# Graph attention on one core: the transposes of the next tile's codes move from before the first unit to after the second

## The reference

```python
# layer 0: h0 = relu(layernorm(x)); two rounds of attention over the neighbours
Wh = h @ W_l
e = leaky_relu(u + v.T + c, 0.2)          # u, v: one number per row
att = softmax(where(adj > 0, e, -9e15), axis=1)
h = 0.2 * h0 + 0.8 * elu(att @ Wh)        # twice, with W[0] and W[1]
x = x + concat([h0, h1, h2]) @ mlp_w + mlp_b
# layer 1: the mean of the neighbours
h = relu(layernorm(x));  a = (adj == 1)
x = x + concat([a @ h / a.sum(1), h]) @ weight + bias
```

## Time and profile before

| what | us |
|---|---|
| median of 3 runs | 1790.13 |
| lowest and highest | 1787.9, 1791.51 |
| the profiled execution | 1792.32 |
| its span, first to last instruction | 1790.5 |

### The profile page before, as it was taken

One profiled execution on the slowest core, in us unless ns is written; L12 is line 12 of the kernel. 1 busy time (PEld: TensorE's weight loads), 2 busy tenths in 40 slices (PEclk: granted clock), 3 DMA queues, 4 the chain that ended last, 5 costly groups with the idle time before them and its releaser, 6 DMA issues. The chain is left out here.

```text
span 1790.5 us, 50269 instructions
## 1 busy us (share of the span) xinstructions
PE 1545.7 (86%) x21779; PEld 1495.5 (84%) x21779; DVE 1565.8 (87%) x2551; ACT 1249.3 (70%) x1341; POOL 144.9 (8%) x164
## 2 busy tenths in 40 slices
PE   2247698888888888888959999999999999799998
PEld 1237688788787878887849999999999999799998
DVE  7689999999999999999989859688696888986675
ACT  3266589898888888888768999999999996000000
POOL 1370000010101010101051000000000000000000
PEclk9668999999999999999979999999999999999999
DMA  7938899999999999999311111111211211133231
GB/s 243 239 144 307 337 362 389 373 380 391 376 405 361 407 367 404 360 407 356 151 43 45 56 44 49 39 59 43 61 55 37 60 31 43 54 102 96 84 96 49
DMA packets 114238, 353.93 MB, mean 198 GB/s; under 512 B 9056, under 2 KB 17248, under 8 KB 114016
## 3 DMA queue, kind: packets, MB, share of 16 engines
q1 hardware_dynamic: 92064, 304.50, 45.5%
q0 software_dynamic: 8512, 27.33, 5.7%
q10 hardware_dynamic: 13440, 18.88, 2.9%
HBM read 323.35 MB, written 27.33 MB: 196 GB/s over the span
## 5 line engine op out<-in xcount | busy, mean ns | idle before, releaser
L475 ACT ACTIVATE region<-ub,bigv 128x1024 uint8<-128x1024 f32 x1024 | 1099.3, 1150 | 81.1 <-DMA x_d<-region 30.9
L1445 PE MATMUL bank<-wsplit,region 128*128 128x195 bf16 x8192 | 791.0, 250 | 62.6 <-DVE region L791 53.8
L1445 PEld LDWEIGHTS bank<-wsplit,region 128*128 128x128 fp8e3 x8192 | 696.6, 99 | 76.4 <-DVE region L791 40.5
L1451 PE MATMUL bank<-wsplit,region 128*128 128x130 f16 x8192 | 558.3, 221 | 58.2 <-DVE region L799 56.9
L1451 PEld LDWEIGHTS bank<-wsplit,region 128*128 128x128 fp8e3 x8192 | 500.5, 98 | 87.7 <-DVE region L799 87.4
L799 DVE SCALAR_TENSOR_TENSOR region<-region 128x512 uint32<-128x512 uint32 x512 | 346.0, 694 | 21.7 <-PE bank L1451 21.0
L791 DVE SCALAR_TENSOR_TENSOR region<-region 128x512 uint32<-128x512 uint32 x512 | 343.1, 699 | 1.4 <-ACT region L475 1.3
L811 DVE TENSOR_SCALAR region<-region 128x4096 uint8<-128x4096 int32 x128 | 293.4, 2292 | 0.1
L1660 PE MATMUL bank<-wsplit,region 128*128 128x129 f16 x4096 | 243.3, 222 | 11.1 <-DVE region L1277 11.1
L1660 PEld LDWEIGHTS bank<-wsplit,region 128*128 128x128 fp8e3 x4096 | 241.0, 99 | 12.6 <-DVE region L1277 12.6
L1277 DVE TENSOR_SCALAR region<-region 128x512 uint32<-128x512 uint32 x256 | 100.4, 424 | 42.7 <-PE bank L1660 37.6
(11 more groups left out here) (183 smaller groups left out, 742.8 us busy)
## 6 DMA issues: line engine op xcount, KB each, us to landing
region<-in_adj SPq DMA_DIRECT2D x128, 2048.0 KB, 11.0
region<-codes_d SPq DMA_DIRECT2D x128, 256.0 KB, 2.7
codes_d<-region ACTq DMA_DIRECT2D x64, 256.0 KB, 6.3
ub<-u_d POOLq DMA_DIRECT2D x16, 512.0 KB, 5.8
hg<-h_d POOLq DMA_DIRECT2D x16, 256.0 KB, 4.8
region<-in_x SPq DMA_DIRECT2D x4, 512.0 KB, 6.3
h_d<-wsplit POOLq DMA_DIRECT2D x4, 512.0 KB, 4.3
x_d<-region POOLq DMA_DIRECT2D x8, 256.0 KB, 16.0
```

What stands on the lines that cost most here:

```text
L475: last = nc.scalar.activation(sv[:, b, :], ub[G % 2][:, :], ACT.Relu, bias=bigv[l][:, t:t + 1], scale=BIG)
L1445: return nc.tensor.matmul(acc_on[it], columns(onb[U % NS], it, b), wsplit[:, c * TC + 2 * q + b, 0:WC], start=(c == 0 and q == 0 and b == ...
L1451: return nc.tensor.matmul(acc_off[it], columns(offb[U % NO], it, b), woff[:, c * TC + 2 * q + b, WO:WO + WF], start=(c == 0 and q == 0 and ...
```

## The change

It moves one call, in the loop over the first layer's tiles. Nothing is added or removed.

```diff
                 for n in range(NT):
                     g, r = n // NCH, n % NCH
+                    unit(0, n, 0)
+                    unit(0, n, 1)
                     if n + 1 < NT:
                         transpose_codes(n + 1)
-                    unit(0, n, 0)
-                    unit(0, n, 1)
                     if n == 1 or (g > 0 and r >= 5) or (g > 1 and r == 0):
                         if n + 1 < NT:
                             pe.wait_ge(p_in, n + 2)
```

## The result

The changed kernel takes 1799.5 us (median of 4, 1799.1 to 1799.9), the kernel before 1789.6 beside it; the ratio is 1.0055, with a 95% interval of 1.0038 to 1.0073. That is 0.4 to 0.7% slower, 6.8 to 13.1 us. The span of the profiled execution grew from 1790.5 to 1798.0 us, 7.5, where the sum said 7.1.

A forecast was written before the change was run, and what follows sets the result against it. VectorE was taken to bound the first layer; 4.9 us at the group ends plus 2.2 at the layer's end gave 7.1, so 1790.1 + 7.1 = 1797.2 us, with 8 in 10 for 1791.5 to 1804.

The forecast's parts named there:

- the sum: Whole kernel: 4.9 us at seven group ends plus 2.2 at the layer's end, 7.1 us slower.
- What bounds: First layer: VectorE sets the time, its waits are paid in full, and at most some 1.3 us can be won.
- The ordinary tile: Most first-layer tiles: later transposes cost nothing, with 3.7 us to spare for the codes and 2.3 for pack_pairs.
- The new wait: 27 tiles: PE resumes 1.73 us after its transposes begin, once ScalarE has copied; 21 cost nothing, except the last two.
- The end of a group: Seven group boundaries: ScalarE reaches the accumulators late, so pack_pairs is 0.73 us late; 0.7 a time, 4.9 in all.
- the boundary is absorbed: Group ends, rival: scaled_sums before E + 0.8 means no pack_pairs wait, only +2.2 at the layer's end, 1792.3; chance 0.24.
- the first wait: Group's first tile: VectorE waits 0.73 us before pack_pairs, hiding a second wait, 0.4 us, for the take of the codes.
- The upper bound: Group ends: ScalarE's copies take 1.6 us longer beside PE's matmuls, 2.3 us a boundary or 16 in all.
- the forecast's lower end: Forecast total with a cost of 0.25 us a boundary: 1793.7 us, in a case given 0.66.
- The end of the layer: Tiles 62 and 63: PE's lag of 0.46 us and a new wait of 1.73 are paid, 2.2 us.
- The clock: Rival: new waits in PE bring its clock down, 1.6 us each; 34 us slower, 1824; chance 0.07.
- The rival's price: Lowered clock in tiles r = 5, 6, 7, 0: 5.7 us less slack of 1.9, or 3.8 a group.

The follow-up runs named there:

- e5: Changed kernel with the old order in the last tile of each group, the first of the next, and tile 62; ratio 1.0007 to the kernel before.
- e3: Changed kernel with the old order in the first tile of each group but the first group; ratio 1.0029 to the kernel before.
- e2: Kernel before, with the new order only in the last tile of each group and the first of the next; ratio 1.0026 to the kernel before.
- e1: Kernel before, with the new order in tile 62 alone; ratio 1.0008 to the kernel before.
- e7: Changed kernel, but ScalarE copies out the small product of r = 0 after emptying the accumulators, not before; ratio 1.0031 to the kernel before.
- e6: Changed kernel with the old order in tile 62 alone; ratio 1.0042 to the kernel before.
- e4: Changed kernel with the old order in the last tile of each group (r = 7); ratio 1.0011 to the kernel before.
- e8: Changed kernel with the next tile's transposes moved between the first and second unit, in all tiles; ratio 1.0007 to the kernel before.

## Why the prediction was right

*What bounds.* Right. VectorE is the clock of this layer, and every idle of it shows in the total: eight idles before line 822 with 0.08 added to each, 5.7 us, and 0.2 at a DMA make up the 5.9 by which the tiles grew.

*The ordinary tile.* Right, in e5: no cost, with all distances in place. ScalarE's idle moved from before line 496 to before line 483.

*The new wait.* Its size was right: 1.12 us at r = 5 to 7, with line 1403 starting 1.72 after the transposes (1.73 said). So was the lag: in tile 39 the transposes came 6.07 into the tile (606.31, with its start at 600.24, 11.02 before 611.26), said 6.04. One place was left out: at r = 0 PE waits longer, 1.94, because ScalarE is late there.

*The end of a group.* Right in mechanism, and in size at six boundaries: they are 0.74 late, said 0.73. That it is so near is luck in part. ScalarE reached the accumulators at E + 1.38, where I had 1.50, and the boundary is absorbed before E + 0.65, where I had E + 0.8; the two errors, 0.1 each, cancel. The take began at E + 10.01 (said 10.37) and ended at 11.15, under the first wait, as said. Without the first wait, in e3, it cost 0.17 to 0.22.

The upper bound, 2.3 a boundary, had 1.6 us in it that last_units lost at one boundary and not at another (4.52 - 2.89), added to ScalarE's copies. With the new order at the boundary no run shows copies that are longer by this: the 16 took 4.47 us in the changed kernel (612.64 to 617.11), and 4.46 in e2 at the boundary where the merged matmuls took 4.53 (612.53 to 616.99).

The first boundary, 1.04 late, was mis-sized. I had taken it as the others, and its clock is another. PE stood still for 3.21 us at the start of tile 7, while VectorE split a block of weights, and did its next matmuls at a low clock, so ScalarE reached the accumulators at E + 1.70:

```profile
215.66 1.79 PE L1445 MATMUL bank<-wsplit,region 128*128 128x195 bf16 x16 [3.21 <-DVE region L791]
```

```profile
216.00:219.00 3.00, 3.00 (x31) 2.96 (x30) 3.00 (x4) 0.47 (x1) 0.00 (x0) 0.62 0.94 385
```

In the kernel before the same three microseconds had a clock of 1.00. But it isn't shown that the change brought the low clock, and two runs speak against it: e1, which has the old order in tile 7, had it too, and e3, with the new order and the same pause of 3.21, did not:

```profile
212.40:215.40 3.00, 3.00 (x25) 2.88 (x24) 3.00 (x3) 1.72 (x2) 0.00 (x0) 0.50 1.03 406
```

```profile
212.28 1.51 PE L1445 MATMUL bank<-wsplit,region 128*128 128x195 bf16 x16 [3.21 <-DVE region L791]
...
212.30:215.30 3.00, 3.00 (x41) 3.00 (x42) 3.00 (x3) 0.79 (x1) 0.00 (x0) 1.00 1.01 412
```

Seven of the ten profiles have the low clock at the start of tile 7, under either order. What it is worth at this boundary is seen in e7, where tile 7 started at full clock: ScalarE came at E + 0.38, the merged matmuls ran at half clock instead (4.53 us after 2.47 of idle, 0.50 from 226 to 228 us), and pack_pairs was 0.57 late, not 1.04.

The eighth wait before line 822, 0.20 us in tile 4, comes after units at a low clock too (2.77 us for the 16 matmuls at 173.26, after 2.96 of idle, with 0.50 granted). So the group ends and this tile cost 5.8 us where I said 4.9. One sum of the prediction is off without consequence: 0.25 a boundary with the 2.2 gives 1794.1 as the forecast's lower end, not 1793.7.

*The end of the layer.* Right in size, 2.19 for 2.2: PE's third unit of tile 62 starts 8.00 into the tile, before 5.80. e1 shows the part of the wait, e6 that of the lag. Wrong in what I said the profile would show: the wait before line 863 did not get longer, it vanished. VectorE's masks came late too (2.35 us before line 791, then three waits of 0.26, 1.28 and 1.32 for ramps) and used up the time that VectorE had to spare. PE's own delay remained, and VectorE came back to it with nothing to spare: its last mask before line 863 started 0.63 us before it.

*The clock.* The prediction's rival was that the new waits bring the granted clock down, at 1.6 us a wait. In the changed kernel the 21 new waits of 1.1 us (seven before line 1397, thirteen before line 1403, one before line 1440) and five of the six longer ones, 1.94 at r = 0, left the granted clock at 1.00, and six of the seven windows of a group had 1.00, where six of seven had 0.98 before. Only the sixth, in tile 40, was followed by 0.50:

```profile
624.00:626.00 2.00, 2.00 (x17) 1.90 (x16) 2.00 (x3) 2.00 (x3) 0.00 (x0) 0.50 1.02 398
```

And the fall at the merged matmuls, six times of seven before the change, came at none of the seven after it. So in the changed kernel one of the 27 new waits was followed by a lower clock. The experiments are less kind to the longer waits at r = 0. The clock fell during the wait or within 1.5 us of it like this:

| run | waits at r = 0 | followed by 0.50 |
|---|---|---|
| changed | six of 1.94 us | 1 |
| e6 | six of 1.94 | 2 |
| e4 | six of 1.94 | 5 |
| e3 | six of 2.38 | 2 |
| e5 | six of 2.38 | 4 |
| e7 | six of 2.57 | 3 |

One of e4's, with a unit's on side at 2.14 us where it takes 1.51 at a granted clock of 1.00:

```profile
615.07 2.14 PE L1445 MATMUL bank<-wsplit,region 128*128 128x195 bf16 x16
...
616.00:618.00 2.00, 2.00 (x18) 1.90 (x17) 2.00 (x5) 2.00 (x3) 0.00 (x0) 0.50 1.03 412
```

No wait before line 822 followed in e4, e5, e6 and the changed kernel; in each of the five cases of e3 and e7 one of 0.2 to 0.5 us did, one tile later. The short waits aren't safe in all company either: in e2 two of the six waits of 1.1 us at r = 7, with 0.84 of idle just behind them, were followed by merged matmuls at half clock (4.53 and 4.45 us). The rival's price, 3.8 us a group, was never seen: no fall behind a new wait at r = 0 cost VectorE more than 0.6 us.

What stays open is why the measured medians differ by 9.9 us, the first layer of the profiles by 8.1 and the whole profiles by 7.5. The spread of the start of the layer, 5 us, is more than these differences, and the interval holds all three.

## What to carry to other kernels

When an engine's duty is moved in its program, list who waits for it by semaphore and when each is due, tile kind by tile kind: here most tiles had two microseconds to spare, and the time went at the group's ends, where an engine off the critical path (ScalarE) had a long job behind the awaited one. Where a wait is removed, look at lengths of tiles too, and not at the list of idles alone: the one that took its place in e3 was too short for the list and was there six times. A wait on the engine that sets the time of a stretch is paid in full, even if another engine was seen waiting there: here eight of them made 5.7 of the 5.9 us by which the tiles grew, and the one at the layer's end cost 1.59 (e1) although VectorE had 3.20 of waiting there. And put a step that another engine must answer so early that the answer is there when it is needed: one unit earlier (e8) the same move cost 0.3 us, for 8.1.

## What the runs showed of the hardware

In these runs TensorE's clock after a pause was not a matter of the pause alone. After 2.57 us of idle 32 matmuls took 4.52 us or 2.89; after 2.51 us in e8 they took 2.88 or 2.89 at all six boundaries; after 0.84 us, in e2, 4.53 at one boundary and 2.89 at another, though at both PE had stood still for 1.1 us just before as well. At the start of tile 7 the clock was 1.00 after 3.21 us of idle in e3 and 0.62 after 3.21 in the changed kernel. So here the same pause was followed by a clock of 0.50 or 0.62 and by one of 1.00, from boundary to boundary and run to run, and a term that rests on it should be given both values.
